# Second layer's routing: table loads moved ahead, twelve weight pieces in flight, four low parts on GpSimd, logits between the last transposes

## The reference, cut to what matters

```
xh    = layernorm(x)                       # input of the mixture
aff   = xh @ centroids.T                   # the logits: 2048 x 8
eid   = argmax(aff, axis=-1)               # one expert for each token
alpha = sigmoid(sum(xh * centroids[eid]))
xn    = layernorm(xh)
xln   = xn * ln_g[eid] + ln_b[eid]
h     = relu(xln @ w1[eid] + b1[eid])      # 256 -> 1024
ffn   = h @ w2[eid] + b2[eid]              # 1024 -> 256
x     = x + tanh(g_ffn[1]) * (xh + alpha * ffn)
```

## Time and profile before

| | us |
|---|---|
| median of 3 runs | 1223.71 |
| lowest and highest | 1221.98, 1230.53 |
| the profiled execution's own time | 1223.31 |
| its span | 1221.6 |
| TensorE busy | 960.7 (79%) |
| VectorE, ScalarE, GpSimd busy | 705.0, 478.4, 473.9 |
| mean granted TensorE clock | 0.879 |

### The profile page before, as it was taken

One profiled execution on the slowest core, in us unless ns is written; L12 is line 12 of the kernel. 1 busy time (PEld: TensorE's weight loads), 2 busy tenths in 40 slices (PEclk: granted clock), 3 DMA queues, 4 the chain that ended last, 5 costly groups with the idle time before them and its releaser, 6 DMA issues. The chain is left out here.

```text
span 1221.6 us, 25288 instructions
## 1 busy us (share of the span) xinstructions
PE 960.7 (79%) x8515; PEld 685.5 (56%) x8524; DVE 705.0 (58%) x1640; ACT 478.4 (39%) x1105; POOL 473.9 (39%) x690
## 2 busy tenths in 40 slices
PE   4888457997576989731999926889988879998898
PEld 3667236996354555521899923355656556556443
DVE  4575435553277567537555546446564464775876
ACT  2363112443122467533343405656663125454110
POOL 1373630775723355403233212556663212432200
PEclk9996668998687999755999976989998799997999
DMA  3364212995401123247677640000000100000000
GB/s 121 92 173 167 89 49 89 370 357 196 142 25 52 54 85 93 84 147 246 233 266 248 230 141 4 1 1 2 1 1 1 52 10 17 25 24 1 18 26 26
DMA packets 68628, 120.89 MB, mean 99 GB/s; under 512 B 14961, under 2 KB 40587, under 8 KB 68523
## 3 DMA queue, kind: packets, MB, share of 16 engines
q1 hardware_dynamic: 61371, 99.93, 24.7%
q0 software_dynamic: 7152, 19.54, 4.8%
HBM read 53.10 MB, written 21.63 MB: 61 GB/s over the span
## 5 line engine op out<-in xcount | busy, mean ns | idle before, releaser
L3693 PE MATMUL bank<-room,xnT 128*128 128x128 bf16 x1104 | 66.8, 221 | 5.9 <-DMA xnT<-l_weights 5.9
L2881 PE MATMUL bank<-l0f_x_high,l_weights 128*128 128x256 bf16 x256 | 49.6, 314 | 26.9 <-issue 14.8
L3693 PEld LDWEIGHTS bank<-room,xnT 128*128 128x128 bf16 x1104 | 64.6, 99 | 7.2 <-DMA xnT<-l_weights 7.0
L3705 PE MATMUL bank<-l_weights,room 128*128 x552 | 65.4, 274 | 3.1 <-DVE keep L3397 1.4
L3096 PE MATMUL bank<-room,l0r_placed 128*128 128x128 bf16 x936 | 59.9, 221 | 0.0
L3445 POOL DMA_INDIRECT l_results<-keep,l1f_slot_target x23 | 22.8, 991 | 93.8 <-DVE keep L3397 93.8
L2087 POOL TENSOR_TENSOR l2x_probs<-l2x_probs,l2x_inverse 128x333 f32<-128x333 f32 x64 | 49.1, 789 | 25.9 <-DVE l2x_inverse L1994 25.9
L3705 PEld LDWEIGHTS bank<-l_weights,room 128*128 128x128 bf16 x552 | 52.4, 97 | 11.6 <-issue 4.3
L3096 PEld LDWEIGHTS bank<-room,l0r_placed 128*128 128x128 bf16 x936 | 56.8, 99 | 0.5
L135 PEld LDWEIGHTS bank<-gate_weights,xnT 128*128 128x128 f32 x256 | 47.6, 281 | 9.4 <-issue 7.1
L135 PE MATMUL bank<-gate_weights,xnT 128*128 128x8 f32 x256 | 46.7, 318 | 6.2 <-PEq L113 3.8
(11 more groups left out here) (488 smaller groups left out, 2725.5 us busy)
## 6 DMA issues: line engine op xcount, KB each, us to landing
xnT<-l_weights SPq DMA_DIRECT2D x23, 1024.0 KB
l0r_placed<-l_weights SPq DMA_DIRECT2D x39, 512.0 KB, 4.7
l_weights<-in_L_ffn_weights SPq DMA_DIRECT2D x16, 512.0 KB, 3.6
l0w_staging<-in_L_ffn_weights SPq DMA_DIRECT2D x16, 480.0 KB, 3.8
room<-l_rows SPq DMA_DIRECT2D x39, 128.0 KB, 4.3
l_results<-room POOLq DMA_DIRECT2D x39, 128.0 KB, 4.4
room<-in_L_ffn_weights SPq DMA_DIRECT2D x8, 512.0 KB, 5.1
xnT<-in_L_ffn_weights SPq DMA_DIRECT2D x8, 512.0 KB, 7.9
```

Source lines behind the costliest of these rows:

```text
L2881: last = pe.matmul(self.bank[:, c, branch * width:(branch + 1) * width], self.weights[w][:, at:at + P], x[:, s, k, :], start=(i == 1), sto ...
L3693: last = pe.matmul(h_bank[u][:, m * P:(m + 1) * P], placed.parts[w][:, u, at:at + P], x[:, u, k, :], start=(s == 1), stop=(s == PARTS * KD))
L3705: last = pe.matmul(bank[:, 2 + u, 0:DIM], h[:, u, c * P:(c + 1) * P], expert_part(split[:, w, :, :], e, KD * hidden_width + c * DIM, DIM), ...
```

## The change

It has four parts.

1. SP issues the four small tables and slot_consts after the first piece of weights and not after the fourth.
2. There are 12 slots and not 8. The four new ones (slots 8 to 11) lie in the part of the tile `weights` that will hold the last four pieces' high and low parts, read as float32; they can be loaded before the logits are ready. ScalarE's high parts go in the order 0 to 3, 8 to 11, 4 to 7, 12 to 15, and before piece 12 it waits until pieces 8 to 11 are split (parts_free), because its output lies over their slots. Pieces 12 to 15 use slots 0 to 3 a second time.
3. GpSimd, after its first four gathers, does the low parts of pieces 11, 3, 7 and 15; VectorE does the other twelve.
4. At the end of the attention one tile of logits stands between the transposes of tiles 12 and 13, and two before those of tile 14, where four stood before those of tile 14. Five tiles are left for the next block, and four were before.

```diff
             logits(5, t + 2 * TPB)
-            for u in range(TPB):
-                norm.tensor(pe, t + 2 * TPB + u)
-            logits(4, t + 3 * TPB)
+            norm.tensor(pe, t + 2 * TPB)
+            logits(1, t + 2 * TPB + 1)
+            norm.tensor(pe, t + 2 * TPB + 1)
+            logits(2, t + 3 * TPB)
             for u in range(TPB):
                 norm.tensor(pe, t + 3 * TPB + u)
...
+    def gpsimd_first(self, pool):
+        pool.wait_ge(self.tokens.source_ready, 1)
+        pool.wait_ge(self.scratch.rows_stored, 16 * BATCH)
+        for j in range(self.AHEAD):
+            self.gather(pool, j)
...
-        chunk, slots, in_room = 1024, 8, 4
+        chunk, slots, in_room, in_parts = 1024, 12, 4, 4
         first = split_before // chunk
         pieces = EXPERTS * per_expert // chunk - first
 
         spare = chip.xnT[:, :, :].rearrange("p k n -> p (k n)")
-        staging = [span_of[:, n * chunk:(n + 1) * chunk] for span_of, many in ((chip.room, in_room), (spare, slots - in_room))
+        late = slots - in_parts, pieces - slots
+        parts = [weights[:, w, (first + slots) * chunk:].bitcast(F32) for w in range(2)]
+        staging = [span_of[:, n * chunk:(n + 1) * chunk] for span_of, many in (
+            (chip.room, in_room), (spare, slots - in_room - in_parts), (parts[0], in_parts // 2), (parts[1], in_parts // 2))
                    for n in range(many)]
+        high_order = [*range(in_room), *range(late[0], slots), *range(in_room, late[0]), *range(slots, pieces)]
+
+        def rounds(q):
+            return len(range(q, pieces, slots))
+
+        def parts_free(eng):
+
+            for q in range(late[0], slots):
+                eng.wait_ge(w_split[q], 1)
...
         def high_part(act, c):
+            if c == slots:
+                parts_free(act)
...
         def room_split(eng):
             for q in range(in_room):
-                eng.wait_ge(w_split[q], pieces // slots)
+                eng.wait_ge(w_split[q], rounds(q))
...
                 sp.dma_start(order[:, :], a["order"].partition_broadcast(P)).then_inc(loaded, 16)
-                for c in range(in_room):
-                    load_weights(sp, c)
+                load_weights(sp, 0)
                 sort.sync(sp, a)
                 tokens.sync(sp, a)
+                for c in (*range(1, in_room), *range(slots - in_parts, slots)):
+                    load_weights(sp, c)
                 sp.wait_ge(logits_ready, 1)
-                for c in range(in_room, slots):
+                for c in range(in_room, slots - in_parts):
                     load_weights(sp, c)
...
             def _(pool):
+                lanes.gpsimd_first(pool)
+                for c in (11, 3, 7, 15):
+                    low_part(pool, c)
                 lanes.gpsimd_loop(pool)
...
-                for c in range(pieces):
+                for c in high_order:
                     high_part(act, c)
                 room_split(act)
...
-                for c in range(pieces):
+                for c in (0, 1, 2, 8, 9, 10, 4, 5, 6, 12, 13, 14):
                     low_part(dve, c)
                 for q in range(slots):
-                    dve.wait_ge(w_split[q], pieces // slots)
+                    dve.wait_ge(w_split[q], rounds(q))
                 dve.sem_inc(weights_ready, 1)
```

More of the change, by code:

```diff
@@ L3434, in sync, with gather @@
         step(self.groups - 1)
-    def gpsimd_loop(self, pool):
[L3437 to L3441, removed]
+    def gather(self, pool, j):
+        wait(pool, self.turned, j - self.AHEAD + 1)
+        pool.indirect_dma_start(out=self.rows[:, j % self.AHEAD, :], out_offset=None, in_=self.scratch.rows,
+                                in_offset=bass.IndirectOffsetOnAxis(ap=self.tokens.source[:, j:j + 1], axis=0)).then_inc(
+            self.rows_loaded[j % self.AHEAD], 16)
+    def gpsimd_first(self, pool):
[3 more added lines that the diff above has]
+            self.gather(pool, j)
+    def gpsimd_loop(self, pool):
         def deliver(j):
@@ L3448, in deliver @@
                 self.stored[j % self.AHEAD], 16)
[L3450 to L3453, removed]
         pool.wait_ge(self.tokens.target_ready, 1)
@@ L3456, in gpsimd_loop @@
             if j + self.AHEAD < self.n:
-                gather(j + self.AHEAD)
+                self.gather(pool, j + self.AHEAD)
             if j >= 1:
@@ L3623, in high_part, with low_part @@
         def high_part(act, c):
+            if c == slots:
+                parts_free(act)
             act.wait_ge(w_loaded[c % slots], 16 * (c // slots) + 16)
             act.activation(high[:, span(first + c, chunk)], staging[c % slots], ACT.Copy).then_inc(w_high_ready, 1)
-        def low_part(dve, c):
-            dve.wait_ge(w_high_ready, c + 1)
-            dve.tensor_tensor(low[:, span(first + c, chunk)], staging[c % slots], high[:, span(first + c, chunk)],
+        def low_part(eng, c):
+            eng.wait_ge(w_high_ready, high_order.index(c) + 1)
+            eng.tensor_tensor(low[:, span(first + c, chunk)], staging[c % slots], high[:, span(first + c, chunk)],
                               ALU.subtract).then_inc(w_split[c % slots], 1)
```

## The result

| | before | after |
|---|---|---|
| median of 20 runs each, us | 1224.96 | 1228.41 |
| lowest and highest, us | 1217.94, 1231.52 | 1223.67, 1233.06 |
| the profiled execution's own time, us | 1223.31 | 1232.28 |

The ratio of after to before is 1.0031, with a 95% interval of 1.0016 to 1.0046: 3.8 us slower, between 2.0 and 5.6. The forecast was no change (1223.5 us, 1218.5 to 1227.5). The measured median lies above the range, and the sign is that of rival (b). The recorded ratio is not the quotient of the medians (which would be 1.0028), and those further down need not be either. One run of e5_logits_alone took 1357.11 us, far above its others, and is left out of its ratio.

The account below looks back on a forecast made before the run. The routing chain ahead of the second layer's expert loop, where TensorE is nearly always busy, was taken to set the time. Terms -2.7, +2.5 and 0.2 summed to 0: forecast 1223.5 us, range 1218.5 to 1227.5.

Parts of the forecast that it names:

- rival (b): Slower: constants' issues on SP are dearer where they now stand; 1225.2 us, or 1228 with tables at half gain; chance 0.2.
- Part 1: Small tables loaded earlier by SP: VectorE's whole wait for them at the head of the routing chain goes, -5.8 us.
- the bounds: Gain from earlier tables: 1.5 us if they land no faster than now, or the whole wait if below 3.7 us.
- Part 2: Logits between the last transposes fill no wait of TensorE; logits ready for the routing 0.1 us later, +0.1.
- Part 3: Twelve pieces in flight: VectorE hardly starved for pieces in its low parts, so more slots save 0.6 us at most.
- Part 4: Four low parts on GpSimd alternate with VectorE's: all split at slot_source + 21.9, -2.7 us including Part 1 and Part 2.
- Rival (a): GpSimd and VectorE don't hinder each other in low parts: 1221.5 us, or 1219 with SP's issues hidden; chance 0.3.
- Part 5: Wait for chip.room: SP's four constant issues fall behind the last low part, ahead of the two copies, +2.5 us.
- 568.0 + 0.3 + 2.5 + 4.6: Forecast start of the first expert matmul, from the low parts' end through constants' issues and copies: 575.4 or so.
- The sum: Routing up to the first expert matmul: -2.7 + 2.5, and 0.2 for one more semaphore, makes 0.

Follow-up runs that it names:

- e5_logits_alone: The kernel before with only the logits moved between the last transposes; ratio to before 0.9982 (0.9962 to 1.0001).
- e4: The changed kernel with the logits at the end of the attentions as before; ratio to before 1.0029 (1.0007 to 1.0051).
- e2: The changed kernel with all 16 low parts on VectorE, none on GpSimd; ratio to before 0.9979 (0.9952 to 1.0006).
- e1: The kernel before with only the four tables and slot_consts issued after the first piece of weights; ratio to before 0.9938 (0.9910 to 0.9966).
- e3: The changed kernel with GpSimd on pieces 11, 7, 6, 5 instead of 11, 3, 7, 15; ratio to before 1.0009 (0.9986 to 1.0032).
- e9: The changed kernel with pieces 12 to 15 loaded into slots 4 to 7, so chip.room is free sooner; ratio to before 0.9988 (0.9966 to 1.0009).
- e8: The changed kernel with pieces 12 to 15 in slots 4 to 7 and all low parts on VectorE; ratio to before 0.9960 (0.9938 to 0.9981).
- e12: e1 with SP loading the first two tiles' four constants behind its wait for the last low part; ratio to before 0.9990 (0.9966 to 1.0013).
- e10: e1 with 40 small matmuls, their output unused, ahead of the first expert matmul; ratio to before 0.9944 (0.9920 to 0.9967).
- e11: e1 with the low parts of pieces 0 and 1 on GpSimd before its gathers; ratio to before 0.9955 (0.9937 to 0.9972).

## Why the prediction was wrong, step by step

- **Part 1, -5.8: right.** Nearness to slot_source 22.84 to 17.08. The choice between the bounds (the whole wait, since the pieces ahead made up the landing) holds.
- **Part 2, +0.1: right.** From the transposes ahead of these logits (507.83 before, 511.36 after) to nearness it is 21.14 us before and 21.08 after; behind nearness e4 shows no cost. e5 shows the earlier start that I had named.
- **Part 3, 0.6 at most: right.** With twelve slots VectorE alone needs 18.41 (e2), with eight 18.91 before and 18.64 in e1.
- **Part 4, all split at slot_source + 21.9: right**, 21.61. The engines take turns: GpSimd's 3.10 is 2.14 and a wait of 0.96, three of VectorE's take 7.05. Rival (a), engines that don't hinder each other, is out. One thing in it was wrong without harm: piece 15 did decide the end, since GpSimd's last part stood 1.74 us for ScalarE's high part of it; e3, with other pieces on GpSimd, is no faster. The Trainium skill ("SBUF — State Buffer", section "Who interferes with whom") calls the two engines' shared ports an exclusive lock and says that the order of issue decides which of the two blocks; the 2.15 us of an instruction of 0.29, started 0.12 us behind GpSimd's, agree.
- **Part 5, the failed step.** The issues were right, the first copy at 2.79 where 0.3 + 2.5 was forecast. What failed is the last term of "568.0 + 0.3 + 2.5 + 4.6": I took the copies' 4.61 us from a place where nothing had been issued just ahead of them, neither constants nor a gather, and it was 6.87. The term for the constants is not +2.5 but +4.8 (2.49 + 2.26). e9 takes 4.27 of it out, e8 4.16, and e12 puts 4.9 into e1 with nothing else of the change. How the 2.26 divide between the constants' transfers and the gather that then goes out ahead of the copies stays open. The sentence that ScalarE's few instructions "fit beside the 4.6 us of the copies" looked at ScalarE and not at the queue, and "so it loses nothing" of GpSimd's next gather did not ask what the copies lose to it. Rival (b) had the sign, but by another price: the issues did not get dearer (0.43 and 0.44), the landing did.
- **The sum.** Forecast 0, measured on the path +1.70 = -5.76 + 2.70 + 2.49 + 2.26, to rounding. With 6.87 for 4.6 the prediction would have read +2.3 and about 1225.8 us, which is still inside the range; that the median lies outside it comes to 1.25 us from the base of three runs and, for the rest, from what follows.

**What stays open.** The time rose by 3.8 us, 2.0 to 5.6, the path by 1.70. The lower end of the interval is nearly there; the rest has no shown cause. In the profiled executions TensorE runs a stretch at half clock in the fourth layer that before does not have. After a pause of 3.36 us its matmuls on 512 columns go from 0.59 for two to 1.06 (granted clock 0.54 from 1142.4 to 1145.4); before, with a pause of 3.08 at the same place, they stay at 0.59 (1.00 from 1133.3 to 1138.0). Before, then after:

```profile
1133.20 0.31 PE L2494 MATMUL bank<-ident,l3f_stack 128*72 128x128 f32 x1 [3.08 <-ACT l3f_stack L2526]
```

```profile
1140.53 0.31 PE L2495 MATMUL bank<-ident,l3f_stack 128*72 128x128 f32 x1 [3.36 <-ACT l3f_stack L2527]
...
1142.39 1.06 PE L2489 MATMUL bank<-l_We_high,l3f_x_high 128*128 128x512 bf16 x2
```

From VectorE's first gates to the end it is 97.90 us in before and 97.89 in e1, but 99.56 in after and 99.56 to 99.58 in each of the other eleven. Three of these (e10, e11, e12) have the code of e1 in this layer, to the last instruction, and e5 has only the logits of the change; so none of the four parts is shown to bring it. The longer stretches in front are no better as evidence. Up to nearness e10 and e11 have the code of before, and take 531.3 and 531.9 us to its 529.0 (after: 532.4). From 129 us behind the first expert matmul to the fourth layer's first logits all kernels have the same code, and those timed near 1225 us take 399.1 to 404.7 us, with 401.2 before and 404.7 after. Each kernel was profiled once, so whether any of this comes with the change or by chance is open.

The best version is e1_tables: 0.9938, better than before and than the change. The ratios of e8, e10 and e11 lie within its interval, so these are not shown to be worse.

## What to carry to other kernels

A wait read from one place holds only with the queue that stood there: when an edit brings small loads right ahead of a copy on the path, or holds the copy back until another queue's transfer goes first, count those transfers and not only the issues. Before work is given to GpSimd beside VectorE, look in the trace for a place where the two already meet; if the later one stands still for the other, each piece moved costs about the difference of the two engines' times (here 0.8 us; 2.14 against 1.14). And time the parts of a change apart: here the tables held the gain, and the low parts on GpSimd and the twelve slots, which move the constants behind the last low part, more than took it back.

## What the runs showed that I had not expected

- The first of two on-chip copies lands 4.6 us after its issue when nothing is right ahead, 5.2 with two small loads ahead, and 6.6 to 6.9 with four and a gather. The four loads run at some 90 GB/s for 3 to 4 us, the copies at 300 to 440.
- Issuing the constants costs 2.5 us of SP's queue wherever it stands; 2.2 us ahead of the copies (e9) is early enough for the landing to be 4.68.
- Forty matmuls right ahead did not bring the next 48 to full clock: 4.45 us where 2.84 is usual.
